# An encoder layer on one core: z and q go through DRAM, and x is loaded one group further ahead

## What is computed

```python
q = (query @ Wq + bq).reshape(b, s, N_HEADS, D_K).transpose(0, 2, 1, 3)
k = (key @ Wk + bk).reshape(b, s, N_HEADS, D_K).transpose(0, 2, 1, 3)
v = (values @ Wv + bv).reshape(b, s, N_HEADS, D_K).transpose(0, 2, 1, 3)
scores = jnp.einsum('bhqd,bhkd->bhqk', q, k) / jnp.sqrt(jnp.float32(D_K))
allowed = j < i + mask                       # mask is 0
attn = softmax(where(allowed, scores, NEG_INF)); attn[:, :, 0, :] = 0
attn_out = (attn @ v, heads joined) @ Wo + bo
x = layer_norm(query + attn_out, ln1_g, ln1_b)
out = layer_norm(x + relu(x @ W1 + b1) @ W2 + b2, ln2_g, ln2_b)
```

## Time and profile before

| what | us |
|---|---|
| median of 3 runs | 1664.28 |
| lowest and highest | 1663.89, 1666.03 |
| the profiled execution | 1661.53 |
| its span, first to last instruction | 1659.6 |
| mean granted TensorE clock | 0.986 |
| busy: PE, ACT, DVE, POOL | 1616.8, 1547.8, 1436.3, 1381.1 |

### The profile page before, as it was taken

One profiled execution on the slowest core, in us unless ns is written; L12 is line 12 of the kernel. 1 busy time (PEld: TensorE's weight loads), 2 busy tenths in 40 slices (PEclk: granted clock), 3 DMA queues, 4 the chain that ended last, 5 costly groups with the idle time before them and its releaser, 6 DMA issues.

```text
span 1659.6 us, 54093 instructions
## 1 busy us (share of the span) xinstructions
PE 1616.8 (97%) x16700; PEld 1590.2 (96%) x16700; DVE 1436.3 (87%) x6746; ACT 1547.8 (93%) x5905; POOL 1381.1 (83%) x1352
## 2 busy tenths in 40 slices
PE   4799999999999999999999999999999999999998
PEld 3699999999999999999999999999999999999997
DVE  3788898898898898898898898898898898898885
ACT  3899999999999999999999999999999999999993
POOL 2378888888888888888888888888888888888896
PEclk7799999999999999999999999999999999999999
DMA  8856665656656656656665666755666656665630
GB/s 153 173 121 119 133 136 117 134 131 120 134 135 117 135 132 119 135 132 119 134 136 116 135 132 118 136 133 116 135 134 117 136 133 118 136 135 117 122 76 27
DMA packets 307087, 208.99 MB, mean 126 GB/s; under 512 B 164336, under 2 KB 281968, under 8 KB 306800
## 3 DMA queue, kind: packets, MB, share of 16 engines
q1 hardware_dynamic: 304960, 204.47, 60.5%
q10 hardware_dynamic: 1840, 1.05, 0.3%
HBM read 104.73 MB, written 50.33 MB: 93 GB/s over the span
## 4 chain that ended last, share of the span: by engine, by line
PE 95%; DVE 2%; ACT 1%; SPq 1%; DMA 1%; issue 0%; POOL 0%; DVEq 0%; ACTq 0%; POOLq 0%
PE ps_dense L393 32%; PE ps_dense L404 32%; PE ps_probsT L500 14%; PE ps_scores L490 7%; PE ps_att L518 7%; PE ps_dense L375 2%; ACT probs L595 0%; DVE ps_scores L804 0%; DMA q_stack<-qT 0%; DMA probs<-in_L_xattn_Wk_dram 0%; SPq L253 0%; PE ps_att L417 0%; SPq L247 0%; SPq L269 0%; SPq L290 0%
## 5 line engine op out<-in xcount | busy, mean ns | idle before, releaser
L595 ACT ACTIVATE probs<-ps_scores,negmax 128x128 f32<-128x128 f32 x2048 | 744.1, 413 | 8.5 <-DVE negmax L804 5.2
L1059 POOL TENSOR_TENSOR probs<-probs,recip 128x512 f32<-128x512 f32 x512 | 533.1, 1042 | 134.7 <-DVE recip L787 134.5
L804 DVE CUSTOM_DVE_ANT_0 ps_scores<-ps_scores,mask 128x128 f32<-128x128 f32 x2048 | 527.0, 318 | 69.9 <-PE ps_scores L490 67.7
L595 ACT ACTIVATION_READ_ACCUMULATOR probs<-ps_scores,negmax 128x1 f32 x2048 | 517.3, 253 | 0.0
L404 PE MATMUL ps_dense<-w,hT 128*128 128x256 f32 x3048 | 417.9, 286 | 0.9 <-DVE u L929 0.9
L393 PE MATMUL ps_dense<-zT,w 128*128 128x256 f32 x3072 | 416.9, 285 | 0.9 <-DVE h_f L888 0.5
L1067 POOL TENSOR_TENSOR hT<-h_f,hT 128x512 fp32r<-128x512 f32 x252 | 322.8, 1294 | 90.4 <-DVE h_f L888 90.4
L393 PEld LDWEIGHTS ps_dense<-zT,w 128*128 128x128 f32 x3072 | 381.8, 189 | 1.5 <-issue 0.9
L404 PEld LDWEIGHTS ps_dense<-w,hT 128*128 128x128 f32 x3048 | 377.5, 188 | 1.2 <-DVE u L929 1.1
L612 ACT ACTIVATE probsT<-ps_probsT 128x508 f32<-128x508 f32 x512 | 319.4, 624 | 37.4 <-PE ps_probsT L500 37.4
L500 PE MATMUL ps_probsT<-ident,probs 128*128 128x128 f32 x2048 | 313.1, 275 | 0.0
(11 more groups left out here) (96 smaller groups left out, 2345.2 us busy)
## 6 DMA issues: line engine op xcount, KB each, us to landing
k_stack<-k_spill SPq DMA_DIRECT2D x384, 128.0 KB, 4.5
q_stack<-qT SPq DMA_DIRECT2D x762, 64.0 KB, 2.0
k_spill<-kT SPq DMA_DIRECT2D x128, 256.0 KB, 2.2
c_tok<-in_ctx_dram SPq DMA_DIRECT2D x256, 64.0 KB, 5.0
x_res<-in_x_dram SPq DMA_DIRECT2D x64, 256.0 KB, 3.0
x_tok<-in_x_dram SPq DMA_DIRECT2D x252, 64.0 KB, 2.4
out_dram<-o_tok SPq DMA_DIRECT2D x63, 256.0 KB, 2.7
probsT<-in_L_xattn_W_dram SPq DMA_DIRECT2D x1, 1024.0 KB, 10.7
```

The costliest lines, as they stand in the source:

```text
L595: last = nc.scalar.activation(probs[:, m % 4, i, :], ps_scores[m % 2][:, i, :], ACT.Exp, bias=negmax[:, m % 4, i:i + 1], scale=-1.0, accum ...
L804: last = nc.vector.tensor_tensor_reduce(ps_scores[m % 2][:, i, :], ps_scores[m % 2][:, i, :], mask[:], -1.0, -MASKED, ALU.add, ALU.min, ac ...
L1059: nc.gpsimd.tensor_tensor(probs[:, m % 4], probs[:, m % 4], recip[:, m % 4, :].unsqueeze(2).broadcast_to([P, 4, S]), ALU.mult)\
```

## The change

- z no longer goes through PE. `spill_z` writes it from `u1` to DRAM, `load_z` reads it back in blocks into the tile of `x_res` (`z_tile`), and `z_flips` turns it there by a block transpose on DVE. `z_hi` and `z_lo` read that tile. The next residual is loaded once `z_lo` is done.
- The last group is the exception: `last_z` transposes it on PE by 16 small matmuls into a bank of scores, inside its first `ff_up`.
- q goes to DRAM (`spill_q`, two DMAs) and back (`stack_q`, three DMAs of 32 partitions) for all groups but group 0, which keeps the 12 DMAs from SBUF.
- The orders of all engines are new. On PE `ff_up` 3 and all four `ff_down` of a group come one iteration later, q is projected three groups ahead instead of two. x is loaded 7 groups ahead in SP's numbering. The banks are dealt anew.
- In front: Wv, Wo and bv are loaded before x of group 1, and v of group 0 is made ahead of the iterations; x of group 3 (the fourth group) is loaded before the rest of the rows and W1. W1, Wo and the norm's two columns are loaded by blocks, to fit the order of z's rows.
- The last group's second norm works in `y_b2` and with the first norm's small tiles.

The diff, cut to its core:

```diff
-ITERATIONS = range(-5, NG + 6)
-BANK = {"zT": 2, "v": 0, "q": 2, "f1_0": 2, "k": 0, "f1_1": 1, "f1_2": 2, "f1_3": 0, "wo": 1, "f2": 1}
-HELD_BY = {"zT": ("q", -3), "f1_0": ("zT", 0), "f1_2": ("f1_0", 0), "q": ("f1_2", 4), "k": ("v", 2),
-        "f1_3": ("k", -3), "v": ("f1_3", 2), "f1_1": ("f2", 1), "wo": ("f1_1", 1), "f2": ("wo", -1)}
+ITERATIONS = range(-7, NG + 6)
+BANK = {"v": 2, "q": 1, "f1_0": 2, "k": 2, "f1_1": 1, "f1_2": 0, "f1_3": 2, "wo": 2, "f2": 0}
+HELD_BY = {"f1_3": ("v", -2), "k": ("f1_3", 4), "f1_0": ("k", -3), "wo": ("f1_0", 1), "v": ("wo", 1),
+        "f1_1": ("q", -4), "q": ("f1_1", 5), "f2": ("f1_2", 0), "f1_2": ("f2", 1)}
...
+            def stack_q0(j):
+                sp.wait_ge(taken["q"], KC)
+                for s, half in enumerate(QPART):
+                    sp.dma_start(f32(q_by_pair[32 * s:32 * s + 32, j]), f32(qT[32 * j:32 * j + 32, half])).then_inc(s_qfirst, 16)
+            def spill_q(g, part):
+                if exists(g) and g > 0:
+                    if part == 0:
+                        sp.wait_ge(s_hi["q"], KC * (g + 1))
+                    else:
+                        sp.wait_ge(taken["q"], KC * (g + 1))
+                    need(sp, s_qstack, 16 * PARTS * (g - 2))
+                    sp.dma_start(q_dram[g % 2, part].rearrange("c p t -> p c t"), f32(qT[:, part])).then_inc(s_qspill[part], 16)
+            def stack_q(g, part):
+                if exists(g) and g > 0:
+                    sp.wait_ge(s_qspill[part], 16 * g)
                     need(sp, s_scores, (g - 1) * UNITS)
                     for s, half in enumerate(QPART):
-                        for j in (2 * i, 2 * i + 1):
-                            sp.dma_start(f32(q_stack[g % 2][32 * s:32 * s + 32, j]),
-                                         f32(qT[32 * j:32 * j + 32, half])).then_inc(s_qstack[i], 16)
+                        if half == part:
+                            sp.dma_start(f32(q_stack[g % 2][32 * s:32 * s + 32]), q_rows[g % 2, part]).then_inc(s_qstack, 16)
...
             def load_residual(g):
                 if exists(g):
-                    if g == 0:
-                        load_weight(5)
-                    need(sp, taken["wo"], g)
+                    need(sp, s_zlo, g)
                     sp.dma_start(x_res[:], x_v[g]).then_inc(s_xres, 16)
+            def spill_z(g):
+                if exists(g) and g < NG - 1:
+                    sp.wait_ge(s_z1, GB * (g + 1))
+                    need(sp, s_zrow, 16 * 4 * (g - 1))
+                    sp.dma_start(z_dram[g % 2].rearrange("b s d -> s b d"), u1[:]).then_inc(s_zspill, 16)
+            def load_z(g):
+                if exists(g) and g < NG - 1:
+                    sp.wait_ge(s_zspill, 16 * (g + 1))
+                    sp.wait_ge(taken["wo"], g + 1)
+                    for j in range(4):
+                        sp.dma_start(z_tile[32 * j:32 * j + 32], z_blocks[g % 2, j]).then_inc(s_zrow, 16)
...
             def iteration(it):                         # SP
-                stack_k(it + 2, 0)
-                next_c(it + 4)
-                stack_q(it + 3, 0)
+                spill_k(it + 3, 0)
+                stack_q(it + 3, 1)
                 load_residual(it + 1)
-                stack_q(it + 3, 1)
-                spill_k(it + 3, 0)
                 spill_k(it + 3, 1)
+                stack_k(it + 3, 0)
+                stack_k(it + 3, 1)
                 store(it - 2)
-                next_x(it + 5)
-                stack_k(it + 3, 1)
+                spill_q(it + 4, 0)
+                next_c(it + 5)
+                spill_z(it + 1)
+                spill_q(it + 4, 1)
+                stack_q(it + 4, 0)
+                load_z(it + 1)
+                next_x(it + 7)
...
+            def last_z():
+                pe.wait_ge(s_z1, GB * NG)
+                pe.wait_ge(s_exp, NG * UNITS)
+                for c in range(KC):
+                    for b in range(GB):
+                        for j in range(4):
+                            first_col = (KC * j + c) * 32
+                            last = nc.tensor.matmul(z_last[32 * j:32 * j + 32, c * GT + b * S:c * GT + (b + 1) * S],
+                                                    u1[:, b, first_col:first_col + 32], ident[:], start=True, stop=True,
+                                                    tile_position=(0, 32 * j), skip_group_check=True)
+                last.then_inc(s_zlast, 1)
...
+            def z_flips(g):
+                if exists(g) and g < NG - 1:
+                    dve.wait_ge(s_zrow, 16 * 4 * (g + 1))
+                    nc.vector.transpose(z_tile, z_tile).then_inc(s_zflip, 1)
```

## The result

The change makes the kernel slower: 1671.44 us median against 1664.09 us in the same runs, a ratio of 1.0048 with a 95% interval of 1.0038 to 1.0058. The prediction said 1644, and that it would be faster. The profiled execution took 1671.82 us, its span 1670.0 us.

The account below looks back on a forecast made before the run. PE was taken to bound the steady part. Fill 105.5 + 60 x 24.43 - 2.9 + drain 71.7 = 1640.1 us of span against 1659.6, so 1664.3 - 19.5 = 1644.8, stated as 1644; range 1634 to 1668.

Parts of the forecast that it names:

- 56 to 59: Fill: the time in us at which group 1's stacks would land, behind x(3), W1, columns and W2.
- all issued by 41.4: Fill: SP's loads ahead of group 1's stacks, about 7 us more of SP time, issued by 41.4 us.
- +1.3 to group 1's scores: Fill: net delay of 1.3 us up to group 1's first scores.
- given back: Fill after group 1's scores: -2.4 us; iteration 2 loses three products (4.3) and a z transpose.
- the first scores of group 3 beyond 110: Fill: sign that the forecast is wrong; 105.5 us was forecast for these scores.
- 4 us either way: Fill: the uncertainty put on the forecast 105.5 us to group 3's first scores.
- 24.87 - 0.44 = 24.43: Steady part: period in us once four z transposes, 0.44 us per iteration, leave PE.
- only change order: Steady part: products, scores and probability transposes stay in number on PE, with no cost counted for their new order.
- the second rival: Middle: DVE or ACT partly bounds, period 24.6 to 24.7, 1656 us; chance 0.20 faster but less, 0.05 within 0.2%.
- the rival with chance 0.23: Middle: DMA latency becomes the bound, stalling PE about 1.0 us per iteration, 1704 us; chance 0.23, slower.
- the stall at the last z: Drain: z_hi, z_lo and their semaphores stand bare because the last z's transpose is behind ff_down(62): 2.2 us.
- POOL's order: Drain: POOL's queue has rstd1(63) ahead of h_lo(62,1), a stall of 1.5 us.

Follow-up runs that it names:

- The short list: Changed kernel with group 1's q spills issued ahead of W1 and the six rows and W2 moved behind group 1's stacks: 1661.27 us, ratio 0.9985.
- The first kernel of the study: Changed kernel with only group 1's two q spills issued ahead of the rows, W1, columns and W2 in SP's queue: 1670.34 us, ratio 1.0048.

## Why the prediction was wrong

**The step that failed** is the fill. The prediction saw that x(3), W1, the columns and W2 stand ahead of group 1's stacks and put their landing at "56 to 59"; they were only issued from 53.3 to 62.5, the k stacks from 59.75, with a median of 4.4 us to landing. It counted the instructions at a pace too fast: "all issued by 41.4", about 7 us more of SP's time, where the list ended at 47.6 (W1 took 3.85, the columns 2.57 and 1.99, W2 2.86). And it never asked what the new spill does in the fill. For the middle it followed each wait of SP's queue; in the fill it followed only the stacks, and not that the one qT tile is held by a spill at the end of that list, with ACT's q_hi, probs and probsT of another group queued behind it. The trace of before had shown the same pattern: ACT stood 10.12 us for q_stack's landing.

"+1.3 to group 1's scores" would have put them at 57.5, and they came at 68.66: 11.1 of the 15.9 us missed. The other 4.8 is "given back" (-2.4), which assumed that iterations 1 and 2 are bound by PE's work. From group 1's first scores to group 3's PE was busy for 4.5 us less than in the kernel before, about the three products counted, but it waited for 14.8 us instead of 8.0, 10.9 of them for ACT's probs and probsT, and the stretch took 52.75 us where it was 50.42. The short list changes little of this: with it PE still waits 12.8 and the stretch is 51.54. What makes ACT late there stays open.

The first kernel of the study shows that the spill was one of several: freeing it alone gave nothing. The kernel with rows and W2 behind group 1's stacks shows that the spill and the list together were the cause of the first part: they gave 11.4 us (10.2 by the medians). The prediction's own sign of a failed fill, "the first scores of group 3 beyond 110", came at 121.4, but no rival was priced for it: both lay in the middle, and the fill had 4 us either way.

**The term mis-sized** is the period: 24.63 where 24.87 - 0.44 = 24.43 stood, 12 us in 60 iterations. The subtraction was right (three of the four transposes gave 0.31, and three quarters of 0.44 are 0.33), and "only change order" at no cost was not. In the two traces the twelve products of an iteration take 16.97 us before and 17.18 after. v's 0.05 of this is shown, by the kernel before with v moved away from q and by two with v moved back; that the rest, some 0.15 us, comes of products that follow others than before, or in k's case of a short wait for a bank, is only argued. Of the last 1.6 us of the 13.6 by which the 60 iterations missed, 1.3 are two waits of PE in the last of them, 0.62 for v's copy and 0.66 ahead of group 63's first scores. It looks like the second rival (24.6 to 24.7), whose number it has, but not its mechanism: taking work from DVE left the period as it was.

**What held.** The first scores at 35.00. No stall by DMA latency: the rival with chance 0.23 did not come, z's spill lands in 2.1 us (2.7 and 4.1 were the bounds) and DVE waits for z's load twice. The DMA share was 0.80, just under the 0.84 forecast, at 173 GB/s or 4.3 MB an iteration where I counted 4.0 (by the earlier trace rows the kernel before moves 129 x 24.87, 3.2 MB and not the 3.0 I started from). The drain was 72.1 against 71.7, with the stall at the last z 1.44 where I had 2.2, and POOL's order 1.3 where I had 1.5. That it fits to 0.4 us is partly luck: PE's waits in it sum to 6.1 us where 8.1 stood, and all the rest took 2.4 us more than counted.

**DVE was mis-sized without harm.** I gave z_lo 0.9 and nothing to its neighbours, 23.1 in all; it is 23.98. By line and shape, between 400 and 1200 us (busy us, mean ns):

```profile
L986 DVE TENSOR_SCALAR var_eps<-mv 128x2 f32<-128x2 f32 x64 | 56.8, 887 | 2.2
...
L889 DVE TENSOR_TENSOR xT<-x_flip,xT 128x512 fp32r<-128x512 f32 x33 | 41.7, 1263 | 0.0
L912 DVE TENSOR_TENSOR zT<-x_res,zT 128x512 fp32r<-128x512 f32 x33 | 41.2, 1248 | 0.0
```

z_lo took 1.25, x_lo 1.26 instead of 1.05, and var_eps, two of two columns each, 0.89 instead of 0.28 us. That is 0.57 + 0.22 + 1.21 us, and 0.68 for the transpose: 2.68, of which the busy time shows 1.8, since records overlap and other lines took less (cT 0.71 instead of 0.82).

## What to carry to other kernels

When a tile's reader becomes a DMA in a queue that works through a list in order, ask for every place of that queue, the fill's as well, who writes the tile next and what stands behind that writer; a forecast for the steady part says nothing of it. In the fill, what the next group's first product needs goes ahead of weights and rows that are used later, and freeing one wait there can be worth nothing, as here, before the list behind it is moved too. Where one engine is busy throughout, a new order of the same work is not free: price it by the neighbours that each piece had and will have, and count the banks' hidden waits before moving a piece back. And compare a figure of the fill with a second profile of the same front before reading an us into it: here two such profiles differ by up to 1.9 us.

## What the runs showed of the hardware

**v's product is faster directly behind q's.** v's twelve matmuls of 128x256 took 1.36 to 1.37 us directly behind q's product, in three kernels and two orders, and 1.41 to 1.42 behind ff_up's or ff_down's, all at the full clock. ff_down's twelve directly behind q's took 1.43. The bank is not the cause: 1.37 was measured in bank 0 and in bank 2. What it is in the pair of q and v, no run tells.

**DVE stands still beside POOL.** The slow DVE operations end with a POOL operation, or 0.55 us behind one: between 400 and 1200 us all 64 of var_eps end within 0.03 us of the end of a POOL operation that was on when they began, and all 33 of z_lo 0.55 to 0.58 behind such a one. DVE's timeline in the changed kernel:

```profile
808.93 0.90 DVE L986 TENSOR_SCALAR var_eps<-mv 128x2 f32<-128x2 f32 x1
...
823.33 1.28 DVE L912 TENSOR_TENSOR zT<-x_res,zT 128x512 fp32r<-128x512 f32 x1
```

And POOL's:

```profile
808.77 1.04 POOL L1135 TENSOR_TENSOR probs<-probs,recip 128x512 f32<-128x512 f32 x1 [0.92 <-DVE recip L856]
...
822.78 1.28 POOL L1198 TENSOR_TENSOR o_tok<-u,g_row 128x512 f32<-128x512 f32 x1
824.14 1.62 POOL L1203 TENSOR_TENSOR o_tok<-o_tok,be_row 128x512 f32<-128x512 f32 x1
```

POOL's product on probs ends at 809.81 and var_eps, a 128x2 operation that took 0.17 us at one place in the trace of before, ends at 809.83. z_lo begins at 823.33, POOL is free at 824.06, and z_lo ends 0.55 us later; POOL's next operation, begun while z_lo was on, takes 1.62 where its neighbours of that shape take 1.28. The Trainium skill (SBUF — State Buffer, "Who interferes with whom") has this as a rule: DVE and GpSimd share one pair of ports under an exclusive lock, and a DVE instruction with two SBUF inputs contends with a GpSimd instruction that reads SBUF. For z_lo the trace agrees, with the numbers above. For z_lo, whose input changed from PSUM to SBUF, the rule would have given an estimated 0.55 to 1.83 us, its own 0.55 and up to one POOL operation of 1.28, and the 1.25 lies between them. I weighed the two rows of L832 instead.

**The list in front issues at different paces.** The same four W1 loads took 3.85 us of SP's queue at 36.12 in the changed kernel, 5.90 at 37.70 with the spill alone ahead of them, and 1.93 at 34.13 with the list shortened; the eight column loads 4.56 and 3.69. The steady part's 0.45 to 0.66 us an issue was too little to count with in the fill: W1's took 0.96 each in the changed kernel. What slows them, no run tells.
